# Residual rows in three buffers instead of a copy on GpSimd, with another order of instructions on all five engines

## The reference

```
x = x + xattn(layernorm(x), ctx, picks)       # 16 heads of 16, 64 picks of 154
h = layernorm(x)
q1, k1, v = h@Wq, h@Wk, h@Wv                  # 8 heads of 64
q2, k2 = h@Wqa@Wqb, softmax(h@Wka@Wkb)        # for the experts
gk1, gk2 = log_sigmoid(gates of h) / 16
e = softmax(h@We); the best of 4 experts takes the row
o = chunked_gla(q1,k1,v,gk1) + sum over experts of chunked_gla(q2*f, k2*f, v, gk2*m)
o = rms_norm(o) * silu(h@Wga@Wgb)
out = x + o @ Wo
```

## Time and profile before

| | before |
|---|---|
| median of 3 runs | 1111.31 us (1107.6 to 1114.18) |
| profiled execution | 1110.09 us, span 1108.8 us |
| granted TensorE clock, mean | 0.982 |
| TensorE busy | 1052.0 us (95%) |
| VectorE busy | 956.1 us (86%) |
| ScalarE busy | 898.9 us (81%) |
| GpSimd busy | 698.4 us (63%) |
| instructions on VectorE / GpSimd | 2793 / 707 |

### The profile page before, as it was taken

How to read it: one execution, slowest core, us unless ns; L and a number is a source line. 1 busy time by engine, 2 the same in 40 slices (tenths; PEclk the granted TensorE clock), 3 DMA queues, 4 the chain that set the end, 5 groups by cost and what they waited for, 6 DMA issues and landing times.

```text
span 1108.8 us, 36916 instructions
## 1 busy us (share of the span) xinstructions
PE 1052.0 (95%) x14912; PEld 871.9 (79%) x14912; DVE 956.1 (86%) x2793; ACT 898.9 (81%) x2259; POOL 698.4 (63%) x707
## 2 busy tenths in 40 slices
PE   4779999999999999999999999999999999999986
PEld 2557888888888888888888888888888888888764
DVE  5679999998999898999989989998999999998652
ACT  3478888888888888888888888888888888888762
POOL 5356666677765666776666667666667766665554
PEclk8689999999999999999999999999999999999999
DMA  6342322232222222223212222222222222121111
GB/s 199 104 127 59 75 55 63 54 87 63 66 69 52 58 67 67 64 67 89 57 47 62 64 63 73 75 61 67 61 57 68 59 70 59 49 60 50 32 32 25
DMA packets 86880, 74.21 MB, mean 67 GB/s; under 512 B 34553, under 2 KB 71743, under 8 KB 86710
## 3 DMA queue, kind: packets, MB, share of 16 engines
q1 hardware_dynamic: 86134, 70.85, 24.2%
q10 hardware_dynamic: 576, 1.02, 0.3%
HBM read 37.43 MB, written 13.94 MB: 46 GB/s over the span
## 4 chain that ended last, share of the span: by engine, by line
PE 73%; DVE 8%; DMA 5%; ACT 4%; POOL 4%; SPq 3%; issue 2%
PE F L410 9%; PE F L873 5%; PE TM L734 5%; PE F L818 5%; PE F L404 5%; PE F L884 4%; PE F L846 4%; PE F L786 4%; PE F L801 3%; PE F L878 3%; PE TM L743 3%; PE F L759 3%; PE F L829 2%; PE F L865 2%; PE SA L722 2%; PE TM L753 2%
## 5 line engine op out<-in xcount | busy, mean ns | idle before, releaser
L729 DVE CUSTOM_DVE_ANT_0 SA<-SA,LNC 128x154 f32<-128x154 f32 x512 | 146.4, 348 | 12.1 <-PE SA L722 12.1
L2128 POOL TENSOR_TENSOR LS<-LS,ZABS 128x512 f32<-128x512 f32 x27 | 47.4, 1755 | 152.0 <-ACT ZABS L1823 152.0
L734 PE MATMUL TM<-CONST,EXPS 128*128 128x128 f32 x512 | 90.0, 299 | 3.8 <-ACT OT L1735 2.3
L715 DVE TENSOR_REDUCE PACKED<-HOT 128x20 int32<-128x1280 bf16 (+1 forms) x64 | 91.7, 1433 | 0.0
L734 PEld LDWEIGHTS TM<-CONST,EXPS 128*128 128x128 f32 x512 | 72.0, 208 | 17.0 <-issue 12.8
L2118 POOL TENSOR_TENSOR LS<-LS,ZABS 128x1024 f32<-128x1024 f32 x27 | 63.9, 2365 | 33.0 <-ACT ZABS L1889 33.0
L729 DVE DVE_READ_ACCUMULATOR2_ANT MAXS<- 128x1 f32 x512 | 72.2, 141 | 0.0
L2143 POOL TENSOR_TENSOR QM<-QD,ISEXPT 128x1024 f32<-128x1024 f32 x27 | 64.1, 2373 | 5.9 <-DMA QD<-QG 5.9
L722 PE MATMUL SA<-KNOW,QS 128*128 128x154 bf16 x512 | 56.5, 233 | 11.0 <-DMA QS<-q_dram 5.9
L2145 POOL TENSOR_TENSOR AT<-AT 128x1024 f32<-128x1024 f32 x27 | 64.4, 2384 | 3.8 <-DVE AT L1460 3.8
L873 PE MATMUL F<-QM,STATE 128*32 128x128 f32 x2048 | 64.0, 278 | 2.5 <-POOL QM L2183 1.9
(11 more groups left out here) (536 smaller groups left out, 3796.8 us busy)
## 6 DMA issues: line engine op xcount, KB each, us to landing
QD<-QG SPq DMA_DIRECT2D x128, 128.0 KB, 2.3
QS<-q_dram SPq DMA_DIRECT2D x64, 192.0 KB, 3.0
q_dram<-QPARTS SPq DMA_DIRECT2D x32, 192.0 KB, 2.5
XA<-x_dram SPq DMA_DIRECT2D x32, 128.0 KB, 2.1
QS<-q_dram SPq DMA_DIRECT2D x32, 128.0 KB, 3.0
XB<-x_dram SPq DMA_DIRECT2D x32, 128.0 KB, 3.4
out_dram<-OUT SPq DMA_DIRECT2D x32, 128.0 KB, 1.7
EG<-EGP SPq DMA_DIRECT2D x128, 4.0 KB, 1.8
```

What stands on the lines that cost most here:

```text
L715: return dve.tensor_reduce(PACKED[:, r], HOT[:, r, :], AX.X, ALU.add)
L729: last = dve.tensor_tensor_reduce(s, s, LNC[t % 2][:, :], -1.0, LARGE, ALU.add, ALU.min, out[:, h:h + 1])
L734: pe.transpose(TA[:, cols(hh)], exps[:, 0:P, hh], ident)
```

## The change

X1 gets a third buffer and X1B goes: OUT reads X1[e % 3], which stays untouched for three turns. The 32 copies of 128 x 256 on GpSimd are gone. All else computes the same with the same instructions. But the programs of all five engines, in all three phases, are written in another order, with semaphores to match.

```diff
-        X1 = two("X1", [P, D])
+        X1 = [sb(f"X1_{i}", [P, D]) for i in range(3)]
...
-        X1B = two("X1B", [P, D])
...
-            dve.tensor_tensor(OUT[:, :], MID, X1B[e % 2][:, :], ALU.add).then_inc(s_e_out, 1)
+            dve.tensor_tensor(OUT[:, :], MID, X1[e % 3][:, :], ALU.add).then_inc(s_e_out, 1)
...
-            dve.wait_ge(s_a_hot, 2 * a + 1)
-            dve.tensor_tensor(HOT[:, :, :], HOT[:, :, :], WEIGHT[:, :].unsqueeze(1).to_broadcast([P, BASES, PICKS]), ALU.mult).then_inc(s_a_hot, 1)
...
-            pool.wait_ge(s_a_qparts, 2 * a + 2)
-            pool.tensor_tensor(QPARTS[:, 2, :, :], QREST[:, :, :], QPARTS[:, 1, :, :], ALU.subtract).then_inc(s_a_qrest, 1)
...
+            pool.tensor_tensor(QPARTS[:, 2, :, :], QREST[:, :, :], QPARTS[:, 1, :, :], ALU.subtract).then_inc(s_a_qrest, 1)
...
-            pool.tensor_copy(X1B[c % 2][:, :], X1[c % 2][:, :])
```

More of the change, by code:

```diff
@@ L887, in pe_first_tiles @@
         def pe_first_tiles(l, a, b, c, d, e):
+            if b == 0:
+                pe_k_rest()
+            if d >= 0:
+                pe.wait_ge(s_d_q1, d + 1)
+                gate_products(LS3[d % 2], CUME[d % 2]).then_inc(s_d_g2_ps, 1)
             if a == 0:
                 pe_k_first()
[L890 to L893, removed]
+            if b >= 0:
+                pe.wait_ge(s_b_exps, 2 * b + 1)
+                scores(b, 1).then_inc(s_b_b, 1)
             if c >= 0:
@@ L915, in pe_first_tiles @@
                 pe.wait_ge(s_a_qt, c + 3)
[L916 to L928, removed]
+                hidden(XMT[c % 2]).then_inc(s_c_hidden_ps_logit_ps, 1)
             if d >= 0:
@@ L982, in pe_first_tiles @@
                 router_rows().then_inc(s_c_rows_ps, 1)
-            if b >= 0:
-                pe.wait_ge(s_b_probs_act, 2 * b + 2)
-                values_pair(b, 2).then_inc(s_b_values, 1)
             if d >= 0:
-                pe.wait_ge(s_d_sq_norm, 2 * d + 1)
-                pe.wait_ge(s_d_states_0, 2 * d + 1)
-                pe.matmul(D2, const("pairs"), RMS[:, :], start=True, stop=True).then_inc(s_d_ms_ps_kvd_ps, 1)
+                pe.wait_ge(s_d_stated, d + 1)
+                state_outputs().then_inc(s_d_o_ps, 1)
             if b >= 0:
@@ L993, in pe_first_tiles @@
             if d >= 0:
+                pe.wait_ge(s_d_sq, d + 1)
+                pe.wait_ge(s_d_states_0, 2 * d + 1)
+                pe.matmul(D2, const("pairs"), RMS[:, :], start=True, stop=True).then_inc(s_d_ms_ps, 1)
                 pe.wait_ge(s_d_states_0, 2 * d + 2)
-                dense_kv_products(V[d % 2]).then_inc(s_d_ms_ps_kvd_ps, 1)
+                dense_kv_products(V[d % 2]).then_inc(s_d_kvd_ps, 1)
             if c >= 0:
@@ L1083, in pe_tiles @@
             values_pair(b, 2).then_inc(s_b_values, 1)
-            pe.wait_ge(s_c_rt, c + 1)
-            pe.wait_ge(s_c_zmin, 2 * c + 2)
+            pe.wait_ge(s_c_router_y, 2 * c + 2)
             router_rows().then_inc(s_c_rows_ps, 1)
+            pe.wait_ge(s_d_sq, d + 1)
+            pe.wait_ge(s_d_states_0, 2 * d + 1)
+            pe.matmul(D2, const("pairs"), RMS[:, :], start=True, stop=True).then_inc(s_d_ms_ps, 1)
+            pe.wait_ge(s_b_ot, 2 * b + 2)
+            transposes(TA, flat(OT[:, :, :]), GROUPS).then_inc(s_b_ot_ps, 1)
+            pe.wait_ge(s_d_states_0, 2 * d + 2)
+            dense_kv_products(V[d % 2]).then_inc(s_d_kvd_ps, 1)
+            pe.wait_ge(s_c_hidk, 16 * c + 16)
+            pe.wait_ge(s_c_hidg, 16 * c + 16)
+            pe.wait_ge(s_c_by_label, c + 1)
+            half_pairs_rows(MIDS, KIDS, WG, HID2, HIDG, WKB, HID1, HIDK).then_inc(s_c_k2_ps, 1)
+            pe.wait_ge(s_b_out, 2 * b + 2)
+            transposes(TA, ON[:, :], KD).then_inc(s_b_ont_ps, 1)
             if a % TPB == 0:
```

1522 lines of the change are left out of this document (766 added, 756 removed).

## The result

The changed kernel takes 1144.12 us (median of 4 runs, 1142.04 to 1146.12); before, 1111.74 (4 runs). The ratio is 1.0304, its 95% interval 1.0283 to 1.0324: 3% slower. The profiled execution took 1142.04 us with a span of 1140.7, 31.9 more than before.

A forecast was written before the change was run, and what follows sets the result against it. It took TensorE as nearly full in the steady part (7.46 us idle of 840) and GpSimd's chain as all but critical. 1110.09 + 13.0 (steady) - 6 (fill) + 1 (drain) = 1118.1, given as 1118, range 1099 to 1132 us.

The forecast's parts named there:

- all else in the steady turns: Steady turns: holes at the turn's head go, -0.23 us a turn; longer turns' excess counted as absorbed, -0.09.
- What bounds the kernel, and the copy: Steady part: TensorE nearly full, GpSimd's chain has 0.5 us to spare; removing the 0.39 us copy is worth nothing.
- HOT x WEIGHT and GpSimd exclude each other: VectorE's 1.45 us multiplication and GpSimd instructions take turns; the later waits for the whole of the other.
- I take the first for four turns of five: Steady turns: HOT x WEIGHT ahead of QM in 0.8 of turns, QM ahead in 0.2; 0.70 us a turn.
- The 1.0 us by which QG2 was to come earlier: VectorE: QG2 no longer behind HOT x WEIGHT, 1.45 us less two instructions on KS; covers XB's load ahead of QD.
- A late EG: SP's queue: XB's load, 0.4 us at most, was taken to cost nothing; no delay of EG was charged.
- The prices: TensorE's stall per steady turn: 0.5 us if HOT x WEIGHT goes first, 1.5 us if QM does.
- QPARTS behind QM: GpSimd, steady turns: later q store and slabs cost 0.4 us in a quarter of turns, 0.1 a turn; bounds 0, 0.7.
- Fill: First tiles: shorter slab waits and pe_v_rest in TensorE's gaps give -6 us; bounds -2 and -10.
- Drain: Last turns: AT ahead of QM delays states and speeds inner outputs, +1 us; bounds 0 to 2.5.
- The rival at 1137: Steady turns: QM first in nearly every turn, +1.2 us a turn, +32, giving 1137 us; chance 0.15.
- The first rival: Steady turns: no collision cost and late slabs fit; about 1098 to 1102 us, say 1100; chance 0.28.

The follow-up runs named there:

- x1_only: Kernel before with three X1 buffers and no copy on GpSimd, all orders old: 1110.29 us, ratio 1.0015.
- before_hot_late: Kernel before with one instruction moved, HOT x WEIGHT put between AT1 and AT2 on VectorE: 1152.87 us, ratio 1.0390.
- dec_back: Changed kernel with ZREST ahead of DEC on GpSimd again: 1126.95 us, ratio 1.0172.
- hot_early: Changed kernel with HOT x WEIGHT back ahead of KS's reciprocal and QG2, and the weights' exponential back on ScalarE: 1139.6 us, ratio 1.0272.
- bhl_delay: before_hot_late with three X1 buffers and a useless 0.4 us GpSimd memset between STATE and the first QM: 1126.37 us, ratio 1.0147.
- qm_delay: Changed kernel with a useless 0.4 us GpSimd memset between STATE and the first QM in each steady turn: 1131.07 us, ratio 1.0171.
- dec_vals: dec_back with VectorE's small VALS moved behind HOT x WEIGHT in the first tiles: 1123.49 us, ratio 1.0119.

## Why the prediction was wrong

Against the profiled execution before, the forecast added 8.0 us and the measurement 31.9. The terms, in us:

| | forecast | measured |
|---|---|---|
| waits for AT2, AT and QM, 27 steady turns | +18.9 (27 x 0.70) | +27.8 |
| waits for slabs of q, 27 steady turns | +2.7 (27 x 0.10) | +9.2 |
| all else in the steady turns | -8.6 (27 x 0.32) | -6.3 |
| fill | -6 | +1.2 |
| drain | +1 | 0 |

The waits were 28.3 and 9.9 us in the changed kernel, and 0.5 and 0.7 before.

- *What bounds the kernel, and the copy*: right. GpSimd's chain of STATE, QM, AT, QM with 0.5 us to spare is where the loss in the steady turns came about, and the copy is worth nothing (x1_only).
- *HOT x WEIGHT and GpSimd exclude each other*: right, with the later one waiting for the whole of the other. The Trainium skill's exclusive lock (SBUF — State Buffer, "SBUF: two separate sides") holds here: 2.24 us of waiting under one QM. The requests were forecast for t = 9.5 and 9.45; they came at 9.37 and 9.25.
- *"I take the first for four turns of five"* is the first step that failed. QM was first in ten of the 27 turns, not in five, and in before_hot_late in eighteen. I had argued from QD landing late "in many turns"; it was late in 11 of 27 before. The turn that I followed is one of these 11. In the other 16 QD landed at t = 8.8 to 9.5, and QM began at 9.4 to 9.55, straight behind STATE; they were the evidence and I let them go. The 1.0 us by which QG2 was to come earlier didn't exist either: K2's reduce went ahead of it, QG2 ended 0.07 us earlier in the turns shown (t = 4.48 for 4.55), and QD lands at 8.8 to 8.9 in the ten turns. What brought QM forward is STATE, which ends at 9.29 instead of 9.58. The right weights at my own prices would have given 23.5 us instead of 18.9.
- *A late EG* was put at nothing, and that is the second step that failed. The order of DEC and ZREST I had seen; that XB's load stands between the moves of EG I had not: the section on the change and the prediction both have it behind all four. Nine turns have a late EG. TensorE waits 9.3 us for AT2, AT and QM in them, 1.0 a turn where I had priced 0.5 or 1.5, and 5.4 us more for slabs of q. They take 33.71 us on the mean against 32.2. dec_back shows that ZREST's wait behind DEC is not the reason, as 33.46 remain without it: STATE is late, and HOT x WEIGHT meets it. hot_early shows that a late STATE without HOT x WEIGHT beside it brings none of these waits but those for slabs. That XB's load makes EG late is read from SP's timeline, and no run moved it back.
- *The prices* were right: QM first 1.5 forecast, 1.3 measured (33.38 - 32.08). TensorE loses it before keys and values, though, where it waits for AT2, and not before the state outputs, where I had looked for it. HOT x WEIGHT first 0.5 forecast: TensorE waits 0.4 a turn for it in the changed kernel (3.3 us in eight turns), which the closed gaps pay for in part, and the turn is no longer than before; it waits 0.5 in bhl_delay, which doesn't have the new head of the turn.
- *QPARTS behind QM*: 0.1 us a turn forecast, 9.9 us in 27 turns measured, 0.37. The term was mis-sized. A late QM is not what made it large, as 8.6 us of these waits remain in qm_delay and 8.8 in dec_back. In the two longest, 1.5 and 1.2 us, the store of q took 3.2 to 3.3 us instead of 2.1, with a packet of instructions among its own. No run put QPARTS back, so how much belongs to its place stays open.
- *Fill*: -6 forecast and -5.9 measured up to the first gate products, of which 1.9 lie ahead of the first scores (23.4 us for 25.3; 22 was forecast). The two turns behind it, +7.1, were left out, the third step that failed. The same collision lies there, but it is a part: with HOT x WEIGHT first in the second of these turns (dec_back) 0.9 us go, and with it first in both (dec_vals) 1.3 more. The other 4.9 stay open. *Drain*: +1 forecast, 0 measured.
- *The rival at 1137* came nearest in its number, and that is luck in part: its +32 for the steady turns was QM first in nearly every turn at 1.2, and the 30.7 measured are ten such turns, nine with a late EG, and slabs. The first rival's own terms add up to 1097.6 to 1099, not to 1098 to 1102.

By kinds the sum is ten turns at 33.75, nine at 33.71 and eight at 32.27 us (slabs' waits included), 899 us for 27 turns; 27 turns before took 868.

## What to carry to other kernels

Before moving a VectorE instruction with two SBUF inputs, look at what GpSimd does at the new place, and price both orders of arrival. When the two requests lie within some tenths of a microsecond, forecast the worse one with at least an even chance: the place is a coin and not a mean. Count over all turns who would be first, and not in one turn. Cost a transfer that stands ahead of a contested instruction with its latest landing, and read the order of the DMA issues line by line, as one load between two moves can make that landing later. And a total can hide a mechanism that was right: hot_early removed the collision in all turns and moved the total by 0.4%.

## What the runs showed of the hardware

- An instruction of GpSimd added on the chain, 0.4 us, made two kernels faster, by 13 and 26 us (medians of different sessions).
- A packet of 16 KB that loads instructions takes one DMA engine for 0.9 to 1.8 us, and moves of 4 KB spread over the engines landed in 3.0 us instead of 1.8 beside one. Where it falls in the turn went together with three kinds of turn from one program.
- With GpSimd's QREST running, VectorE's HOT x WEIGHT starts on record 0.03 us before GpSimd's AT, and AT went first. With STATE running and HOT x WEIGHT waiting for 0.9 us (dec_back), HOT x WEIGHT went first.
- The memset of qm_delay, which reads no tile, overlapped HOT x WEIGHT by 0.3 us in the ten turns, and neither was longer for it (0.42 and 1.45 us).
